# Context attention of a two-layer decoder: another order of the pieces of a frame

## The reference

```python
def _L1_xattn_ref(query, key, value, Wq, Wk, Wv, Wo, bo):
    q = split_heads(query @ Wq.T)
    k = split_heads(key @ Wk.T)
    v = split_heads(value @ Wv.T)
    q = _apply_rope(q)
    k = _apply_rope(k)
    logits = jnp.einsum('bhqd,bhkd->bhqk', q, k) * scale
    attn = jax.nn.softmax(logits, axis=-1)
    out = jnp.einsum('bhqk,bhkd->bhqd', attn, v)
    out = out.transpose(0, 2, 1, 3).reshape(b, t, d)
    return out @ Wo.T + bo
...
x = x + _L1_xattn_ref(_layernorm(x, axis=-1), ctx_1024, ctx_1024, ...)
```

## Time and profile before

| what | before |
|---|---|
| median of three runs | 3329.14 us |
| lowest, highest | 3320.31, 3334.44 us |
| profiled execution, its own time | 3325.31 us |
| its span, first to last instruction | 3323.4 us |
| PE busy, share of the span | 90% |
| DVE busy | 71% |
| ACT busy | 50% |
| frames of this block, first to last L1898 | 1909.8 to 2565.7 us |

### The profile page before, as it was taken

How to read it: one execution, slowest core, us unless ns; L and a number is a source line. 1 busy time by engine, 2 the same in 40 slices (tenths; PEclk the granted TensorE clock), 3 DMA queues, 4 the chain that set the end, 5 groups by cost and what they waited for, 6 DMA issues and landing times. The chain is left out here.

```text
span 3323.4 us, 78589 instructions
## 1 busy us (share of the span) xinstructions
PE 2990.8 (90%) x28488; PEld 2114.3 (64%) x28488; DVE 2356.1 (71%) x4873; ACT 1677.9 (50%) x3240; POOL 838.2 (25%) x1093
## 2 busy tenths in 40 slices
PE   7998999999999996999999599999998799993992
PEld 6886565565555654666788366666665677772771
DVE  5997567666666664676888466666664599994887
ACT  3776455555555552332555244444443588782551
POOL 0000344444444441000000100000000124445771
PEclk9998999999999997999999799999998899995996
DMA  7000444444444540000000233332331578775677
GB/s 184 16 0 2 145 150 146 136 135 135 149 147 146 149 143 2 1 0 1 1 0 0 54 68 68 68 68 60 68 68 27 170 216 232 219 226 175 198 205 257
DMA packets 316577, 351.63 MB, mean 106 GB/s; under 512 B 104536, under 2 KB 290016, under 8 KB 316224
## 3 DMA queue, kind: packets, MB, share of 16 engines
q1 hardware_dynamic: 176128, 175.06, 20.0%
q10 hardware_dynamic: 127216, 139.94, 14.2%
q0 software_dynamic: 13008, 33.56, 3.0%
HBM read 109.49 MB, written 207.08 MB: 95 GB/s over the span
## 5 line engine op out<-in xcount | busy, mean ns | idle before, releaser
L1094 ACT ACTIVATE x_probs<-x_held,x_minus_top 112x488 f32<-112x488 f32 x256 | 177.5, 694 | 281.4 <-DVE x_minus_top L1148 281.4
L1876 DVE TENSOR_REDUCE x_top<-x_scores 112x2 f32<-112x750 f32 x256 | 231.0, 934 | 119.0 <-PE x_scores L1733 114.6
L771 POOL TENSOR_TENSOR x_rstd<-x_var,g_minus_half 112x1 f32<-112x1 f32 x128 | 74.1, 579 | 744.6 <-DVE x_var L767 744.6
L970 POOL TENSOR_TENSOR x_probs<-x_probs,x_inverse 112x488 f32<-112x488 f32 x256 | 250.6, 1000 | 10.0
L1009 PE MATMUL x_ring<-w_xkv,x_kv 128*122 128x512 f32 x512 | 242.3, 596 | 1.2 <-PEq L231 1.2
L1002 PE MATMUL x_ring<-x_kv,w_xkv 128*128 128x488 f32 x512 | 234.7, 592 | 1.8 <-ACT x_kv L1069 1.1
L1142 DVE SCALAR_TENSOR_TENSOR x_held<-x_scores,x_keep 112x976 f32<-112x976 f32 x128 | 150.3, 1174 | 109.2 <-PE x_scores L1022 101.0
L965 POOL TENSOR_TENSOR x_inverse<-x_sums,x_minus_one 112x2 f32<-112x2 f32 x128 | 94.6, 739 | 420.2 <-ACT x_probs L1094 420.2
L1842 ACT ACTIVATE x_probsT<-x_scores 125x1792 f32<-125x1792 f32 x96 | 159.8, 1664 | 79.2 <-PE x_scores L1752 79.2
L1733 PE MATMUL x_scores<-x_slots 32*112 32x375 f32 x1024 | 171.5, 538 | 28.0 <-DVE x_top L1876 14.2
L771 POOL TENSOR_TENSOR a_rstd<-a_var,g_minus_half 112x1 f32<-112x1 f32 x64 | 35.6, 556 | 560.8 <-DVE a_var L767 560.8
(11 more groups left out here) (417 smaller groups left out, 7524.9 us busy)
## 6 DMA issues: line engine op xcount, KB each, us to landing
expert_slots<-d_empty ACTq DMA_DIRECT2D x32, 3612.0 KB, 13.4
by_position<-r_by_position SPq DMA_DIRECT2D x64, 784.0 KB
r_bias<-by_position SPq DMA_DIRECT2D x64, 392.0 KB
m_rows<-expert_slots SPq DMA_DIRECT2D x143, 129.0 KB
x_kq_swapped<-x_kq_raw ACTq DMA_DIRECT2D x64, 243.5 KB, 3.5
x_slots<-x_kq SPq DMA_DIRECT2D x512, 30.4 KB
m_rows<-expert_replies SPq DMA_DIRECT2D x32, 448.0 KB, 7.8
w_ctx<-in_ctx SPq DMA_DIRECT2D x32, 375.0 KB
```

The lines of the kernel that those rows point to most:

```text
L970: self.nc.gpsimd.tensor_tensor(probs, probs, self.inverse[0:T, u:u + 1].to_broadcast([T, XK]), ALU.mult).then_inc(self.weighted, 1)
L1094: nc.scalar.activation(self.probs[u % 6][0:T, :], self.held[m % 2][0:T, i, :], ACT.Exp, scale=self.scale, bias=self.minus_top[0:T, m % 2, ...
L1876: nc.vector.tensor_reduce(self.top[0:T, g, 2 * half:2 * half + 2], self.scores[0:T, 1024 * half:1024 * (half + 1)].rearrange("t (a c) -> t ...
```

## The change

The list of pieces gets another order. All pieces and their ages stay; the score pieces keep their order among themselves. Moved are back0 (ahead of q and tr1), v1 and ctx0 (ahead of onT and g3), ctx1 and xT (g3 and h3 now stand side by side, then xT, ctx1), and v2 (behind put and project). `bank_free` now works its counts out from the list instead of having them written out. For the exponentials it gives b * 3 + i at tr, and (b - 1) * 3 or (b - 1) * 3 + 2 at g and h; for the maxima b * 4 + g, and (b + 1) * 4 + 2 or + 4 at tr. Those are the counts that stood there before. At g and h the wait for the exponential now stands ahead of the wait for the maximum.

```diff
-        self.plan = Flow(4, [("g0", 3), ("h0", 3), ("headsB", 5), ("g1", 3), ("h1", 3), ("k0", 1), ("stats", 0),
...
-                             ("k1", 1), ("g2", 3), ("h2", 3), ("onT", 5), ("ctx0", 0), ("g3", 3), ("ctx1", 0), ("h3", 3),
...
+                             ("v0", 2), ("scale", 0), ("back0", 5), ("q", 1), ("tr1", 4), ("back1", 5), ("k1", 1), ("g2", 3),
+                             ("h2", 3), ("v1", 2), ("ctx0", 0), ("onT", 5), ("g3", 3), ("h3", 3), ("xT", 0), ("ctx1", 0),
+                             ("rope", 1), ("tr2", 4), ("put", 3), ("project", 5), ("v2", 2), ("headsA", 4)],
...
     def bank_free(self, pe, name, b):
 
-        if name[0] in "gh":
-            g = int(name[1])
-            at_least(pe, self.maxed["gh".index(name[0])], b * HG + g)
-            at_least(pe, self.exped, (b - 1) * CC + (2 if g > 1 else 0))
-        else:
-            i = int(name[2])
-            at_least(pe, self.exped, b * CC + i)
-            n = (b + 1) * HG + (HG if i == 2 else 2)
-            for half in range(2):
-                pe.wait_ge(self.maxed[half], min(n, self.NB * HG) if isinstance(b, int) else n)
+        plan = self.plan
+        users = [n for n in plan.names if n[0] in "gh" and n[1:].isdigit() or n[0:2] == "tr"]
+        at = users.index(name)
+
+        def last(kind):
+            k = next(k for k in range(at - 1, at - 1 - len(users), -1) if users[k][0] == kind)
+            return int(users[k][-1]), b + plan.age[name] - plan.age[users[k]] - (k < 0)
+
+        i, before = last("t")
+        at_least(pe, self.exped, before * CC + i + 1)
+        for half in (range(2) if name[0] == "t" else ("gh".index(name[0]),)):
+            g, before = last("gh"[half])
+            done = before * HG + g + 1
+            at_least(pe, self.maxed[half], min(done, self.NB * HG) if isinstance(b, int) else done)
```

More of the change, by code:

```diff
@@ L1629, in __init__ @@
         super().__init__(nc, G, W)
-        self.plan = Flow(4, [("g0", 3), ("h0", 3), ("headsB", 5), ("g1", 3), ("h1", 3), ("k0", 1), ("stats", 0),
[3 rows of a table removed]
-                             ("headsA", 4)],
+        self.plan = Flow(4, [("g0", 3), ("h0", 3), ("headsB", 5), ("g1", 3), ("h1", 3), ("k0", 1), ("stats", 0), ("tr0", 4),
+                             ("v0", 2), ("scale", 0), ("back0", 5), ("q", 1), ("tr1", 4), ("back1", 5), ("k1", 1), ("g2", 3),
+                             ("h2", 3), ("v1", 2), ("ctx0", 0), ("onT", 5), ("g3", 3), ("h3", 3), ("xT", 0), ("ctx1", 0),
+                             ("rope", 1), ("tr2", 4), ("put", 3), ("project", 5), ("v2", 2), ("headsA", 4)],
                          bankless=("tr0", "tr1", "tr2", "g0", "h0", "g1", "h1", "g2", "h2", "g3", "h3", "rope", "stats", "scale"),
```

## The result

The change takes 3343.48 us (median of 6 runs, 3341.75 to 3346.01) against 3329.11 us of the kernel before (6 runs, 3320.31 to 3334.44). The ratio is 1.0045, with a 95% interval from 1.0032 to 1.0059. The forecast was 3335 us in a range of 3317 to 3348: the side was right. The forecast step was +6 us against +14.4 measured, so its size was less than half of what came.

The account below looks back on a forecast made before the run. PE's queue and the score banks were taken to bound the frame; +0.25 us a frame, less up to 0.05 in front, over about 27 frames gave +6 us, a median of 3335 us in a range of 3317 to 3348.

Parts of the forecast that it names:

- two chains of nearly the same length: In each frame, PE's queue and the four score banks; a new order helps only if it shortens both.
- Tr2 to tr0: Frame's start, with put and project ahead of v2: kept at 9.71 us, costing nothing.
- the paragraph on `bank_free`: Reordered waits at g and h: put at nothing, at most 0.05 us at g2, +1.4 us in all.
- Tr0 to g2: back0 ahead of tr1 makes tr1 and then g2 0.24 us later, g2 at 15.88 us after tr2.
- g2 to g3: v1, ctx0 (0.35 us, an estimate) and onT precede g3, which starts at 18.38 us instead of 17.57.
- g3 to tr2: PE ready at about 20.1 us, but tr2 waits for both maxima until 21.14, including 0.05 us to hand over.
- the front part: From tr2, put needing less time there than v2 did: up to 0.05 us shorter a frame, an estimate.
- the draining frames: The block's last frames, without ctx0, xT and ctx1: left at nothing, having little of what was moved.
- frames up to 0.76 us longer: Upper bound for the frame: ctx0 at 0.75 us and 0.16 us to hand over.
- PE alone: Rival: only PE's time sets the frame, saving about 1.0 us each, 27 us in all, 3302 us; chance 0.14.
- The delay of g3 by its ring banks or by a long ctx0: Slower rival: g3 starts 0.4 us later still, up to +0.76 us a frame, 3349 us; chance 0.13.
- The clock: Part of the slower rival: one idle microsecond a frame lowers PE's clock, costing several us a frame; chance 0.03.

Follow-up runs that it names:

- e8: The change, with the maxima of index 3 taken over 187 of the 375 context columns: frame 20.49 us, ratio 0.9961.
- e6: The kernel before with ctx1 moved from between g3 and h3 to in front of g3, old bank_free: frame 20.45 us, ratio 0.9967.
- e1: The kernel before, old order of pieces, with the new bank_free: frame 21.08 us, ratio 1.0029.
- e2: The change's new order of pieces with the old bank_free: frame 21.18 us, ratio 1.0019.
- e3: The change with back0 put back behind tr1: frame 21.06 us, ratio 1.0000.
- e7: The change with bank_free's waits the other way round, maxima first and exponential last: frame 21.09 us, ratio 1.0019.
- e5: The change with back0 put back behind tr1 and v1 behind ctx1: frame 20.90 us, ratio 1.0009.

## Why the prediction was right, and where its size was off

What bounds the frame, right: two chains of nearly the same length, PE's queue and the score banks. e8 shows the second by shortening it alone, from the change, where it was the longer one; e6 gains from the kernel before because it shortens both.

Tr2 to tr0, forecast 9.71 and measured 9.76. put in front of v2 saves 0.05, as was guessed; but the pair g1 h1 costs 0.09 more than before, 2129.40 - 2127.83 = 1.57 us. The step that failed is the paragraph on `bank_free`: "I put it at nothing", or at most 0.05 us at g2. It costs nothing at g2 and 0.09 to 0.10 at h1; e1 and e2 price it at 0.10 us a frame in this order and 0.19 in the old one.

Tr0 to g2, right: 6.15 us where before it was 5.93, so +0.22 us, forecast +0.24, for back0 in front of tr1; e3 takes back the 0.22.

g2 to g3, right: 2.50 us as forecast, with ctx0 near its short end (0.32 us).

g3 to tr2, the mechanism right, one term off: the hand-over from the last maximum to tr2. I took 0.05 us, from an exponential and g2, and had 0.16 as the other end; it is 0.15. A tr waits for three semaphores. In the change an instruction of its own holds the two for the maxima, and the first weight load carries the one for the exponential; in e7 the load carries the one for the maximum of h, and tr2 starts 0.06 us after it. The loads of tr2 in the change and in e7 show it in the same way as those of h1:

```profile
2142.34 0.99 PEld L1751 LDWEIGHTS x_scores<-x_q,x_slots 32*125 32x125 f32 x32 [1.15 <-issue]
```

```profile
2076.32 0.96 PEld L1751 LDWEIGHTS x_scores<-x_q,x_slots 32*125 32x125 f32 x32 [1.18 <-DVE x_top L1879]
```

I had taken the 0.16 before for PE being busy, and the row could not tell the two apart: with 0.15 us for the hand-over itself, both chains ended within about 0.02 us of each other there.

The sum was +0.25, less 0.05 for the front part; measured +0.39. 0.25 - 0.05 + 0.10 (hand-over) + 0.09 (h1) = 0.39, to the 0.01 or 0.02 us of such readings. So the measured frame is the forecast one with two terms of waiting that were taken too small. Over 27 frames that is 10.5 us instead of 6.

The rest of the +14.4 us of the medians is settled only in part. In the profiled executions it takes 12.1 us longer from the first tr2 to the last: the 25 full frames outside the round's beginning make +9.4 (the first two less than 0.39 each, since before they were 0.1 us longer than the rest), the frame where the second round begins -0.7, the first step +0.6, and the last four steps, 78.3 us before (2498.38 to 2576.68) and 81.1 after (2509.03 to 2590.12), +2.8. So the draining frames, which I had left at nothing, cost almost 3 us in this pair. Their rows, before and after (length, busy us of PE, PEld, DVE, ACT, POOL, clock share, DMA share, GB/s):

```profile
2498.38:2576.68 78.30, 65.58 (x965) 44.33 (x965) 36.33 (x58) 28.20 (x35) 0.00 (x0) 0.87 0.12 21
```

```profile
2509.03:2590.12 81.09, 66.71 (x965) 46.02 (x965) 36.78 (x58) 27.45 (x34) 0.00 (x0) 0.85 0.11 20
```

The same four steps take 77.8 us at a granted clock of 0.87 in e3, 83.0 at 0.82 in e1 and 82.8 at 0.81 in e5: in these traces they are longer where the clock is lower, and in e1 they can hold what its frames don't explain. That is read from one execution each; no run changed it on its own. Outside the block the pair differs too, by 2.5 us ahead of the first add and 3.0 behind the last, and the kernel before alone scatters over 14 us. The total of +14.4 stayed inside the range by its upper end, which was meant for frames up to 0.76 us longer; the forecast itself had nothing for this rest, so there it was luck.

The rivals: PE alone does not decide, since tr2 waits 0.95 us for DVE; the gain for PE was there, 1.18 us for g3 and h3 instead of 1.63, and went into that wait. The delay of g3 by its ring banks or by a long ctx0 did not happen. The clock held 1.00 in the full frame above, and likewise from 2300 to 2321 and from 2400 to 2421 us, so an idle microsecond a frame did not lower it. While the block drains it did fall: after 1.30 us of idle time in front of tr2,

```profile
2529.99 2.04 PE L1751 MATMUL x_scores<-x_q,x_slots 32*125 32x112 f32 x32 [1.30 <-DVE x_top L1879]
2531.96 1.01 PE L1739 MATMUL x_ring<-g_constants,x_top_wide 112*128 112x112 f32 x4
```

```profile
2530.00:2534.00 4.00, 4.00 (x41) 3.58 (x42) 3.96 (x5) 1.66 (x1) 0.00 (x0) 0.58 0.02 4
```

tr2 held PE for 1.97 us instead of 1.07, at a granted clock of 0.58, mostly the lower level of 1.2 GHz. The Trainium skill (TensorE: Matmul & The Clock Gate, Part 1) says that idle gaps between bursts bring the clock down; this stretch agrees, and the frame of 2121 to 2142 us shows that a gap of 0.95 us in each frame does not. It is not the work of the change: in the kernel before the clock fell in the draining frames too, where a tr0 behind 1.32 us of idle time held PE for 2530.28 - 2528.55 = 1.73 us. And in the changed kernel a tr0 behind 1.23 us held it for the usual 1.07 (2541.15 to 2542.22). Which gap is too much can't be read from these cases, and was not tried.

## What to carry to other kernels

When two chains share a resource in a cycle, place a piece by what it delays on the other chain, not by the time that it saves on its own: work belongs where the engine would wait anyway (ctx1 in front of g3 in e6), and not where it holds back the next use of a bank that is already free (v1 in front of g3, back0 in front of tr1). Where an instruction waits for several semaphores, let it carry the one that comes last; the others are better waited for ahead of it. A frame read from the trace to 0.01 us settles such questions long before the runs' scatter of some us lets the total do it; what filling and draining cost it does not tell (almost 3 us here).

## What the runs showed of the hardware that I had not expected

The hand-over from a maximum on DVE to the next score matmul takes 0.05 to 0.06 us when the matmul's own weight load carries the wait that ends last (h1 and g3 before and in e6, tr2 in e7), and 0.15 us when that wait is an instruction of its own in front of it (h1 and g3 in e1, h1 and tr2 in the change). It makes no difference there whether this instruction waits for one maximum (h1) or for both (tr2). Equal counts in another written order changed the frame by 0.19 us, in e1 as in e7.
